# A four-layer graph network on one core: another order of the work ahead of the scatter, two ScalarE chunks in each fourth group, and another opening of the last layer

## The chip, the core and the metric

The kernel runs on one core of a Trainium2 chip. A core has five engines that work side by side: TensorE (PE in the rows, with its weight load PEld), VectorE (DVE), ScalarE (ACT), GpSimd (POOL) and SyncE (SP, here the queue that issues most DMAs). They meet only at semaphores: an instruction waits until a counter has reached a value that others raise. The metric is the device time of one execution in microseconds (us), lower is better.

## The reference, cut to what matters

625 nodes with 512 features, 20,000 edges. Each of four layers is `x = x + layer(relu(layernorm(x)))`.

```python
h = jnp.maximum(_layernorm(x), 0.0)
x = x + L0(h)   # GCN: deg by edge weight; agg = segment_sum(h@W_conv [src] * norm, dst); @ W_lin + b_lin
h = jnp.maximum(_layernorm(x), 0.0)
x = x + L1(h)   # SAGE: mean over incoming edges; h = mean @ W_l + b + x @ W_r; h * sigmoid(h)
h = jnp.maximum(_layernorm(x), 0.0)
x = x + L2(h)   # 4 blocks: conditioned norm, sparse attention (4 heads), conditioned norm, MLP
h = jnp.maximum(_layernorm(x), 0.0)
x = x + L3(h)   # GAT forward and backward (4 heads each), concat, @ W_fuse, batch norm, relu
```

The attention of L3 is, per direction, `e = leaky_relu(a_s[src] + a_d[dst], 0.2)`, a softmax over the edges of each target, and the weighted sum of `h[src]`. The conditioning of L2 comes from `silu(emb @ f_w1 + f_b1) @ f_w2 + f_b2`, with sines and cosines of node_vec1 in emb.

## The kernel before

The nodes lie in five tiles of 128 (NT = 5), the features in four (KT = 4). Matrices are kept as a high and a low part (fp32r), and a product of two of them is three matrix products.

**Ahead of the scatter** (span 0 to 34 us). DVE takes layer norm tile by tile: statistics, `first_norm(t)` (L2457), then PE turns the tile (`turn_first`, L1820), ACT makes the high part (`first_turned`, L1652), DVE the low part (`first_rest`, L2463), and PE multiplies it by W_conv (`own_features`, L1796; the last raises `big_full` for `hall`). In between, DVE adds two bias rows (L2514), splits the edge weights into three bf16 parts `w_part` (five operations, L2517 to L2520), and copies the identity into the accumulator (L2531, L2532). POOL makes the angles of the sines (L1433 to L1449, six steps on tile mask), the reciprocal deviations (`rstd_of`, L1409 and L1411), the low part of W_conv (`rest(Q_CONV)`, L1416), then adds the bias row to all five tiles of x (L1464), and clears paddings (L1469, L1472). ACT also makes sine, SiLU and high parts of weights.

**The scatter loop** (34 to 118 us). The edges come in NG = 40 groups of 512, each of CH = 4 chunks of 128. They become a dense 640 x 628 adjacency (weights and counts) by products of one-hot matrices in bf16. For a group, DVE makes the one-hot rows of the sources for three chunks (L2543, 128x628) and the one-hot rows of the targets (L2545, hot_dst), ACT the fourth chunk (Abs L1682, then Relu L1684), POOL multiplies hot_dst by the three weight parts (L1483, three operations), PE makes 60 small products (L2081, L2084), and DVE adds the result to the accumulator (L2554). HOT = 4 buffers turn, so DVE makes group n+3 and then adds group n. The loop body in code holds four groups, b = 0 to 3.

**Behind it**, DVE makes the two adjacencies and the degrees; POOL makes low parts of L1's left weights (L1416) and the power of the degrees (L1498), then the reciprocal deviations of L1's layer norm (L1409, L1411), for which DVE waits in its norm (L2457).

**The last layer** (785 to 890 us). PE makes the hidden features of both directions, `hidden(t)` (12 products, L1796), which ACT copies (L659). Then a loop over 8 heads and 5 source tiles (40 items): DVE combines two branches to scores (L1040, and L1003 for the row maxima), POOL and ACT make the exponentials (L632, L757), PE sums (L925, 4 products for an item). `target_rows(p)` turns four target rows for two heads (L843, ACT copies them at L669 and L675), `second_branch`, `first_branch` and `maxima` spread them over the partitions (L818). `idle_products(pe, bank, n)` makes n products of a tile of ones that nobody reads (L1807). PE's order here is written out by hand; `hidden(4)` comes last ahead of the loop.

SP loads L1's weights (Q_LEFT, Q_RIGHT) in pairs left and right; the first two of Q_RIGHT go to slots of the tile bias and wait for the adds of L1464.

## Time and profile before

| | us |
|---|---|
| median of 3 runs | 902.62 |
| lowest, highest | 901.32, 902.70 |
| the profiled execution | 900.32 |
| its span | 898.6 |
| PE busy | 837.1 (93%) |
| DVE busy | 644.9 (72%) |
| POOL busy | 516.5 (57%) |
| ACT busy | 459.7 (51%) |

The profile shows one execution. Times in its rows are from the start of the span; 1.7 us of the execution lie outside the span. Busy shares are means over stages with different limits, so a stage is read from its own stretch. An "x3" row holds three instructions in a row with one time from the first start to the last end; neighbouring instructions on an engine overlap a little at their ends, so the start of the next row is the better measure of what one costs. PEclk is the TensorE clock that was granted, 1.00 for 2.4 GHz and 0.50 for 1.2 GHz; its mean is 0.988.

### The profile page before, as it was taken

Reading aid. Unit: us, or ns where it says so; the run is one execution under the profiler, and the core shown is the slowest. Engines: PE = TensorE matmul, PEld = TensorE weight load, DVE = VectorE, ACT = ScalarE, POOL = GpSimd, SP = SyncE. Lnnn points to the kernel's source line nnn. Section 1 sums busy time; section 2 is a strip of 40 time slices with the busy share of each in tenths; the row PEclk is TensorE's granted clock in tenths of the full one; section 3 lists DMA queues with packets and bytes.
Section 4 is the critical chain, followed back from the end, with each engine's and each line's share of the span. In section 5 each row is a group of like instructions: output and inputs, shape, how many; then the busy total and the mean of one; then the engine's idle time right before and its main releaser. Section 6 shows DMA issues by size and latency. Waiting matters only on the chain.

```text
span 898.6 us, 18329 instructions
## 1 busy us (share of the span) xinstructions
PE 837.1 (93%) x6775; PEld 732.6 (82%) x6775; DVE 644.9 (72%) x1274; ACT 459.7 (51%) x771; POOL 516.5 (57%) x622
## 2 busy tenths in 40 slices
PE   3899999999999999999999999999999999998797
PEld 2798877779898878989887989888898988875466
DVE  8899988885575774476667366577546667689986
ACT  4787757244674233476134456424346634155664
POOL 7777744469532666743367853266684338447871
PEclk9999999999999999999999999999999999989989
DMA  5100011133200133300015310013230002100121
GB/s 135 37 0 0 0 48 26 60 102 110 59 2 5 31 109 91 109 13 2 12 44 159 89 54 12 1 36 98 81 113 20 1 1 83 36 1 31 45 60 58
DMA packets 49761, 44.34 MB, mean 49 GB/s; under 512 B 6013, under 2 KB 37439, under 8 KB 49698
## 3 DMA queue, kind: packets, MB, share of 16 engines
q1 hardware_dynamic: 47234, 39.72, 15.2%
q10 hardware_dynamic: 2464, 3.80, 1.5%
q8 instruction: 38, 0.62, 0.3%
q14 instruction: 25, 0.20, 0.1%
HBM read 42.04 MB, written 1.33 MB: 48 GB/s over the span
## 4 chain that ended last, share of the span: by engine, by line
PE 70%; DVE 16%; ACT 6%; issue 4%; DVEq 2%; POOL 1%; DMA 0%; SPq 0%; ACTq 0%
PE psum L1796 20%; PE psum L1790 18%; PE psum L1901 12%; PE psum L1871 6%; PE psum L1820 5%; PE psum L925 3%; DVE arena L2321 3%; ACT arena L1598 2%; PE psum L1844 2%; PE psum L866 1%; DVEq L2550 1%; DVE z L2543 1%; DVE arena L1003 1%; DVE stats L2444 1%; DVE hot_dst L2545 1%
## 5 line engine op out<-in xcount | busy, mean ns | idle before, releaser
L1345 POOL TENSOR_SCALAR acc<-acc,rden,flag 128x628 f32<-128x628 f32 x80 | 69.4, 868 | 119.4 <-DVE rden L2317 119.4
L1901 PE MATMUL psum<-ringw,arena 128*128 128x512 f32 (+1 forms) x480 | 119.3, 397 | 4.0 <-DVE arena L2329 2.5
L1796 PE MATMUL psum<-arena 128*128 128x384 f32 (+5 forms) x675 | 115.9, 325 | 1.1 <-DVE hot_dst L2694 1.1
L1790 PE MATMUL psum<-arena,ringw 128*128 128x314 f32 x768 | 114.2, 310 | 0.1
L1790 PEld LDWEIGHTS psum<-arena,ringw 128*128 128x128 f32 x768 | 112.9, 190 | 1.4 <-DVE arena L2294 1.1
L1796 PEld LDWEIGHTS psum<-arena 128*128 128x128 f32 (+1 forms) x675 | 104.9, 189 | 8.1 <-DVE hot_dst L2694 1.5
L1901 PEld LDWEIGHTS psum<-ringw,arena 128*128 128x128 f32 (+1 forms) x480 | 86.9, 186 | 25.6 <-DVE arena L2329 3.5
L1790 PE MATMUL psum<-arena 128*128 128x314 f32 (+1 forms) x480 | 87.8, 321 | 7.3 <-DVE arena L2321 6.7
L1790 PEld LDWEIGHTS psum<-arena 128*128 128x128 f32 (+1 forms) x480 | 70.4, 187 | 15.8 <-DVE arena L2321 14.1
L1416 POOL TENSOR_TENSOR ringw<-raw,ringw 128x512 fp32r<-128x512 f32 x56 | 71.7, 1291 | 19.3 <-ACT ringw L1639 15.4
L2294 DVE SCALAR_TENSOR_TENSOR arena<-psum,cols,arena 128x628 fp32r<-128x628 f32 x32 | 27.9, 871 | 70.6 <-ACT arena L1580 70.5
L1820 PE MATMUL psum<-ident,acc 128*128 128x128 f32 (+1 forms) x528 | 75.3, 274 | 0.2
L2321 DVE TENSOR_TENSOR arena<-psum,arena 128x640 fp32r<-128x640 f32 x80 | 65.0, 817 | 14.5 <-ACT arena L1598 14.5
L1416 POOL TENSOR_TENSOR ringw<-xn,ringw 128x512 fp32r<-128x512 f32 x49 | 64.9, 1329 | 16.2 <-ACT ringw L1639 16.1
L1483 POOL TENSOR_TENSOR hot_dst<-hot_dst,w_part 128x160 bf16<-128x160 bf16 x120 | 58.2, 512 | 26.2 <-DVE hot_dst L2545 26.2
L1593 ACT ACTIVATE acc<-acc,nsmax 128x628 f32<-128x628 f32 x80 | 65.2, 815 | 13.3 <-DVE nsmax L2312 12.9
L1820 PEld LDWEIGHTS psum<-ident,acc 128*128 128x128 f32 (+1 forms) x528 | 61.7, 140 | 8.0 <-DVE arena L2294 1.2
L1409 POOL TENSOR_SCALAR veps<-mv 128x1 f32<-128x1 f32 x60 | 13.6, 227 | 90.7 <-DVE mv L2448 89.0
L2312 DVE CUSTOM_DVE_ANT_0 acc<-psum,mask 128x628 f32<-128x628 f32 x80 | 63.7, 801 | 0.0
L1529 ACT ACTIVATE arena<-psum 128x512 fp32r<-128x512 f32 x40 | 23.8, 594 | 73.8 <-PE psum L1820 58.9
L1796 PE MATMUL psum<-arena,ringw 128*128 128x314 f32 x384 | 58.5, 310 | 2.3 <-DVE arena L2211 2.3
L1871 PE MATMUL psum<-ringw,arena 128*128 128x512 f32 x240 | 58.7, 395 | 0.9 <-DVE arena L2211 0.6
(310 smaller groups left out, 1907.0 us busy)
## 6 DMA issues: line engine op xcount, KB each, us to landing
raw<-in_L_gnn_m_w SPq DMA_DIRECT2D x16, 256.0 KB
xn<-in_L_gnn_m_w SPq DMA_DIRECT2D x16, 256.0 KB
raw<-in_L_gnn_wv SPq DMA_DIRECT2D x8, 256.0 KB
xn<-in_L_gnn_wv SPq DMA_DIRECT2D x8, 256.0 KB
raw<-in_L_gnn_wq SPq DMA_DIRECT2D x8, 256.0 KB
xn<-in_L_gnn_wq SPq DMA_DIRECT2D x8, 256.0 KB
raw<-in_L_gnn_wk SPq DMA_DIRECT2D x8, 256.0 KB
xn<-in_L_gnn_wk SPq DMA_DIRECT2D x8, 256.0 KB
```

Source lines behind the costliest of these rows:

```text
L1345: g.tensor_scalar(pbuf[:, k % 4, 0:NW], pbuf[:, k % 4, 0:NW], rden[:, k:k + 1], flag[:, 1, k % NT:k % NT + 1], ALU.mult, ALU.mult).then_in ...
L1416: g.tensor_tensor(to[1], staged[slot(n)], to[0].bitcast(F32), ALU.subtract).then_inc(split_done, 1)
L1483: ins = g.tensor_tensor(hot_dst[:, b, :, (i + 1) * WIN:(i + 2) * WIN], hot, w_part[:, i, :, bass.ds(gr, 1)].broadcast_to([P, CH, WIN]), AL ...
L1593: act.activation(pbuf[:, k % 4, 0:NW], pbuf[:, k % 4, 0:NW], ACT.Exp, bias=nsmax[:, k:k + 1], scale=-1.0, accum_out=den[:, k:k + 1]).then_ ...
L1790: ins = pe.matmul(big[buf(u)][0:l.shape[1], h, 0:HW], l, r[:, h * HW:(h + 1) * HW], start=(i == 0), stop=(i == len(terms) - 1))
L1796: ins = pe.matmul(to, l, r, start=(i == 0), stop=(i == len(terms) - 1))
L1820: ins = pe.transpose(bflat(u)[0:KEYS[k], k * P:(k + 1) * P], src[:, k * P:k * P + KEYS[k]], ident[:, :])
L1871: ins = pe.matmul(brow(u), l, r, start=(k == 0 and i == 0), stop=(k == KT - 1 and i == 2))
L1901: ins = pe.matmul(brow(ROWBLK[f"{name}{t}"])[0:KEYS[t], :], l, r, start=(pieces[0] + i == 0), stop=(pieces[-1] == KT - 1 and i == len(term ...
L2294: dve.scalar_tensor_tensor(wide(to[:, 1, h, :]), bwide(u), bqk[:, i, bass.ds(it * KT + h, 1)], wide(f32(to[:, 0, h, :])), ALU.add, ALU.sub ...
L2312: dve.tensor_tensor_reduce(wide(pbuf[:, k % 4, :]), bwide(u), wide(mask[:, t, :]), -DH ** -0.5, 3e38, ALU.add, ALU.min, nsmax[:, k:k + 1]) ...
L2321: dve.tensor_tensor(pT[:, 1, :, t * P:(t + 1) * P], bflat(u).rearrange("p (k n) -> p k n", k=NT), f32(pT[:, 0, :, t * P:(t + 1) * P]), ALU ...
```

## The change

Five parts.

- **A, order ahead of the scatter.** DVE splits the weights right after `first_norm(3)`, ahead of the bias addition, `first_rest(2)` and `first_norm(4)`. The copies of the identity go to ACT, which also makes ones_r and two high parts ahead of `first_turned(2)`. DVE no longer waits for `hall` ahead of its loop, and does the small pick operation (L2576) before the loop instead of behind it. POOL makes `rest(Q_CONV)` ahead of the third and fourth rstd_of, and the five bias additions to x move behind the loop: two behind `left_rest(0, 1)`, three behind `left_rest(2, 3)`, ahead of L1's `rstd_of`. PE turns the last tile after `own_features(1)`, makes z1, then `own_features(2)` to `(4)`, and 2 products of ones instead of 4. SP loads L1's weights in another order, the first of Q_RIGHT into z.
- **B, the scatter loop.** In the group b = 3 ACT makes two chunks and DVE two (instead of one and three); a third scratch lies in xn.
- **C.** Products of ones: 6 instead of 7 behind the loop, 3 instead of 1 at L1's third tile.
- **D, the opening of the last layer.** The products of ones (1, 3 and 3) go. `hidden(4)` is made in two halves in their place, ahead of `second_branch(0)` and `second_branch(1)`; ACT copies Hf3 ahead of `second_branch(1)` and Hf4 behind it; 5 products of ones instead of 6 ahead of the loop.
- **E, the last layer's loop.** Four times 4 products of ones, one ahead of `target_rows(3)`'s wait and one behind each ACT read of target rows at n = 5, 15, 25.

```diff
-        hot_abs = [mask[:, NT - 1, :].bitcast(BF16)[:, b * NP:(b + 1) * NP] for b in range(2)]
+        def own_chunks(b):
+            return CH - 1 - (b == HOT - 1)
+        hot_abs = [... for b in range(2)] + [xn[:, 1, D - NP // 2:D].bitcast(BF16)]
...
             second_branch(0)
+            hidden("f", 3)
             second_branch(1)
-            for t in range(3, NT):
-                hidden("f", t)
+            hidden("f", 4)
...
+                if p == NJ // 2 - 1:
+                    idle_products(pe, 0, 4)
                 pe.wait_ge(c_up, 2 * p + 2)
...
-            pe.wait_ge(h_read, 2 * NT - NROW)
-            spare = 2 * NBIG + ROW3[f"Hf{NT - 1}"] % NROW
-            idle_products(pe, spare, 1)
             target_rows(0)
-            idle_products(pe, spare, 3)
+            hidden(4, range(0, KT // 2))
             second_branch(0)
-            idle_products(pe, spare, 3)
+            hidden(4, range(KT // 2, KT))
...
             first_branch(1)
-            hidden(4)
-            idle_products(pe, 2 * NBIG, 6)
+            idle_products(pe, 2 * NBIG, 5)
...
+                for p in range(1, NJ // 2):
+                    if n == 2 * NT * p - 5:
+                        pe.wait_ge(misc_read, MISC[f"vt{p}"] + 1)
+                        idle_products(pe, 0, 4)
...
+            g.wait_ge(dstep, 9)
             step(g.tensor_tensor(r, part, ph, ALU.add))
...
             rstd_of(2, 2)
+            rest(Q_CONV, ringpart(Q_CONV))
+            rstd_of(3, 3)
...
             for k in range(2):
                 left_rest(k)
+            for t in range(2):
+                bias_added(t)
             g.wait_ge(w_up, 1)
...
             for k in range(2, KT):
                 left_rest(k)
+            for t in range(2, NT):
+                bias_added(t)
...
+                        for j in range(own_chunks(b), CH):
+                            act.activation(hot_abs[n][:, 0:NW], iota16[:, 0:NW], ACT.Abs, ...)
+                            act.wait_ge(hot_abs_up, ...)
+                            ins = act.activation(hot_src[b][:, j, 0:NW], hot_abs[n][:, 0:NW], ACT.Relu, ...)
+                        ins.then_inc(hot_act_up, 1)
...
-            dve.wait_ge(big_full, BIG0["hall"] + 1)
...
-                    for j in range(CH - 1):
+                    for j in range(own_chunks(b)):
```

How the instructions stand on DVE from the last layer norm tiles to the loop; xn is the normed tile, w_part the split weights, the rows at L2543 and L2572 the first one-hot chunks. Before:

```order
L2514 TENSOR_TENSOR bias<-psum,bias 128x512
L2463 SCALAR_TENSOR_TENSOR arena<-psum,arena 128x4x128
L2457 TENSOR_SCALAR xn<-x,mv,rstd 128x512
L2517 CAST w_part<-edge_col 128x160
L2519 TENSOR_TENSOR edge_col<-edge_col,w_part 128x160
L2520 CAST w_part<-edge_col 128x160
L2519 TENSOR_TENSOR edge_col<-edge_col,w_part 128x160
L2520 CAST w_part<-edge_col 128x160
L2463 SCALAR_TENSOR_TENSOR arena<-psum,arena 128x4x128 x2
L2531 COPY acc<-ident 128x4x128
L2532 COPY acc<-ident 128x128
L2537 TENSOR_LOAD span_i
```

After:

```order
L2546 CAST w_part<-edge_col 128x160
L2548 TENSOR_TENSOR edge_col<-edge_col,w_part 128x160
L2549 CAST w_part<-edge_col 128x160
L2548 TENSOR_TENSOR edge_col<-edge_col,w_part 128x160
L2549 CAST w_part<-edge_col 128x160
L2556 TENSOR_TENSOR bias<-psum,bias 128x512
L2498 SCALAR_TENSOR_TENSOR arena<-psum,arena 128x4x128
L2492 TENSOR_SCALAR xn<-x,mv,rstd 128x512
L2498 SCALAR_TENSOR_TENSOR arena<-psum,arena 128x4x128
L2561 TENSOR_TENSOR pick<-fcol,pick 128x1
L2498 SCALAR_TENSOR_TENSOR arena<-psum,arena 128x4x128
L2566 TENSOR_LOAD span_i
```

The five operations on the weights stand ahead of the last norm now, and the two copies are gone from this engine.

On POOL behind the scatter loop, from the low parts of L1's left weights (ringw) to the first reciprocal deviation. Before:

```order
L1416 TENSOR_TENSOR ringw<-raw,ringw 128x512 x2
L1498 TENSOR_TENSOR degs<-degs,half 128x2
L1498 TENSOR_TENSOR degs<-degs,half 128x3
L1416 TENSOR_TENSOR ringw<-raw,ringw 128x512 x2
L1409 TENSOR_SCALAR veps<-mv 128x1
```

After:

```order
L1434 TENSOR_TENSOR ringw<-raw,ringw 128x512 x2
L1484 TENSOR_TENSOR x<-x,bias 128x512 x2
L1520 TENSOR_TENSOR degs<-degs,half 128x2
L1520 TENSOR_TENSOR degs<-degs,half 128x3
L1434 TENSOR_TENSOR ringw<-raw,ringw 128x512 x2
L1484 TENSOR_TENSOR x<-x,bias 128x512 x3
L1427 TENSOR_SCALAR veps<-mv 128x1
```

Two additions stand ahead of the power, three ahead of the first deviation.

On PE in the opening of the last layer; 128x256 are hidden features, 36x128 the turned target rows, 128x314 from arena the spread branches, ones_r the products of ones, and hot_dst the first item of the loop. Before:

```order
L1796 MATMUL psum<-ringw,arena 128x256 x12
L1807 MATMUL psum<-ones_r 128x512
L843 MATMUL psum<-ident,iota 36x128 x5
L1807 MATMUL psum<-ones_r 128x512 x3
L818 MATMUL psum<-arena 128x314 x2
L1807 MATMUL psum<-ones_r 128x512 x3
L818 MATMUL psum<-arena 128x314 x8
L1796 MATMUL psum<-ringw,arena 128x256 x12
L1807 MATMUL psum<-ones_r 128x512 x6
L925 MATMUL psum<-hot_dst,acc 128x314 x4
```

After:

```order
L824 MATMUL psum<-ringw,arena 128x256 x12
L857 MATMUL psum<-ident,iota 36x128 x5
L824 MATMUL psum<-ringw,arena 128x256 x6
L830 MATMUL psum<-arena 128x314 x2
L824 MATMUL psum<-ringw,arena 128x256 x6
L830 MATMUL psum<-arena 128x314 x8
L1840 MATMUL psum<-ones_r 128x512 x5
L938 MATMUL psum<-hot_dst,acc 128x314 x4
```

The twelve products of the fifth tile stand where six of the products of ones stood, and between the last spread and the first item only five products of ones are left.

## Rows read from the trace of the kernel before

**Rows 1.** The page: the chain that ended last, by engine.

```profile
PE 70%; DVE 16%; ACT 6%; issue 4%; DVEq 2%; POOL 1%; DMA 0%; SPq 0%; ACTq 0%
```

**Rows 2.** Timeline of DVE ahead of the scatter: start, us, engine, line, operation, [idle before, releaser].

```profile
23.27 0.23 DVE L2517 CAST w_part<-edge_col 128x160 bf16<-128x160 f32 x1
...
23.89 1.21 DVE L2520 CAST w_part<-edge_col 128x160 bf16<-128x160 f32 x1
...
27.58 0.68 DVE L2463 SCALAR_TENSOR_TENSOR arena<-psum,arena 128x512 fp32r<-128x512 f32 x1
28.99 0.69 DVE L2463 SCALAR_TENSOR_TENSOR arena<-psum,arena 128x512 fp32r<-128x512 f32 x1 [0.73 <-ACT arena L1652]
29.59 1.01 DVE L2531 COPY acc<-ident 128x512 f32<-128x512 f32 x1
...
33.72 0.97 DVE L2543 TENSOR_SCALAR mask<-iota,edge_col 128x628 bf16<-128x628 f16 x3 [2.92 <-issue]
```

**Rows 3.** Timeline of POOL ahead of the scatter.

```profile
21.54 1.28 POOL L1416 TENSOR_TENSOR ringw<-raw,ringw 128x512 fp32r<-128x512 f32 x1
...
23.62 6.41 POOL L1464 TENSOR_TENSOR x<-x,bias 128x512 f32<-128x512 f32 x5
```

**Rows 4.** Timeline of PE ahead of the scatter, and its first product of the loop.

```profile
22.97 2.05 PE L1796 MATMUL psum<-ringw,arena 128*128 128x256 f32 x8 [1.89 <-DVE arena L2463]
...
30.30 2.16 PE L1796 MATMUL psum<-ringw,arena 128*128 128x256 f32 x16
...
37.07 0.20 PE L2081 MATMUL psum<-hot_dst,mask 128*128 128x80 bf16 x1 [3.67 <-ACT z L1684]
```

**Rows 5.** Timeline of DVE in the scatter loop: its start, and single operations of one steady group.

```profile
35.92 0.58 DVE L2545 TENSOR_TENSOR hot_dst<-iota,edge_col 128x160 bf16<-128x160 f16 x1
...
96.57 0.58 DVE L2543 TENSOR_SCALAR z<-iota,edge_col 128x628 bf16<-128x628 f16 x1
97.07 0.31 DVE L2545 TENSOR_TENSOR hot_dst<-iota,edge_col 128x160 bf16<-128x160 f16 x1
97.31 0.56 DVE L2554 TENSOR_TENSOR acc<-psum,acc 128x400 f32 x1
```

**Rows 6.** Timeline of POOL in that group: its third product.

```profile
96.43 0.54 POOL L1483 TENSOR_TENSOR hot_dst<-hot_dst,w_part 128x160 bf16<-128x160 bf16 x1
```

**Rows 7.** Timeline of ACT: two one-hot pairs at the loop's start, without a wait.

```profile
33.81 0.80 ACT L1682 ACTIVATE mask<-iota,edge_col 128x628 bf16<-128x628 f16 x1
...
35.28 0.80 ACT L1682 ACTIVATE mask<-iota,edge_col 128x628 bf16<-128x628 f16 x1
```

**Rows 8.** Stretches of the scatter: us, busy (x count) of PE, PEld, DVE, ACT, POOL, PEclk, DMA share, GB/s.

```profile
38.40:41.40 3.00, 3.00 (x73) 3.00 (x70) 3.00 (x8) 1.54 (x2) 2.39 (x6) 0.50 0.00 0
45.00:53.00 8.00, 7.41 (x252) 7.22 (x248) 8.00 (x21) 6.69 (x10) 5.65 (x12) 1.00 0.00 0
```

**Rows 9.** Timelines of POOL, DVE and PE at L1's layer norm.

```profile
131.00 0.19 POOL L1409 TENSOR_SCALAR veps<-mv 128x1 f32<-128x1 f32 x1 [2.40 <-DVE mv L2448]
...
132.69 0.51 DVE L2457 TENSOR_SCALAR xn<-x,mv,rstd 128x512 f32<-128x512 f32 x1
...
137.93 0.66 PE L1820 MATMUL psum<-ident,xn 128*128 128x128 f32 x4 [1.06 <-DVE xn L2457]
```

**Rows 10.** Timeline of PE in the last layer's opening.

```profile
805.35 2.90 PE L1807 MATMUL psum<-ones_r 128*128 128x512 f32 x6 [0.56 <-ACT acc L659]
```

**Rows 11.** Timeline of DVE in the last layer: the waits for PE.

```profile
810.07 0.87 DVE L1040 SCALAR_TENSOR_TENSOR hot_dst<-psum,edge_col,bias 128x628 f32<-128x628 f32 x1 [2.57 <-PE psum L925]
...
860.09 0.87 DVE L1040 SCALAR_TENSOR_TENSOR raw<-psum,edge_col,bias 128x628 f32<-128x628 f32 x1 [0.37 <-PE psum L925]
...
868.42 0.87 DVE L1040 SCALAR_TENSOR_TENSOR raw<-psum,edge_col,bias 128x628 f32<-128x628 f32 x1 [0.19 <-PE psum L925]
```

**Rows 12.** Timeline of PE in the last layer's loop: the last of its long waits.

```profile
853.12 1.62 PE L925 MATMUL psum<-hot_dst,acc 128*128 128x314 f32 x4 [2.04 <-ACT z L693]
```

**Rows 13.** A stretch of the last layer's loop, columns as in rows 8.

```profile
854.00:861.00 7.00, 7.00 (x15) 4.17 (x14) 6.59 (x7) 3.75 (x6) 5.42 (x3) 0.52 0.42 128
```

More of the change, by code:

```diff
@@ L505, in slot, with place @@
             return (n - S_COND) % STAGE if n >= S_COND else n % OUTER
+        def place(n):
+            return z[:, NT - 1, :] if n == Q_RIGHT[0] else staged[slot(n)]
         def ld_count(n):
@@ L805, in hidden_and_own, with hidden @@
                        sum([parts(tile_of(yT, k, t), [wb[:, s, k, :] for s in range(2)]) for k in range(KT)], [])).then_inc(h_full, 1)
-            def hidden(t):
+            def hidden(t, ks=range(KT)):
                 u = ROW3[f"Hf{t}"]
-                pe.wait_ge(h_read, NT + t - NROW + 1)
-                pe.wait_ge(split_done, S_L3 + 4)
+                if ks[0] == 0:
+                    pe.wait_ge(h_read, NT + t - NROW + 1)
+                    pe.wait_ge(split_done, S_L3 + 4)
                 def weight(k):
                     return [r[:, (k % 2) * w:(k % 2 + 1) * w] for r in ringpart(RING_L3 + k // 2)]
-                row_mm(pe, brow(u)[:, 0:w], sum([parts(tile_of(yT, k, t), weight(k)) for k in range(KT)], [])).then_inc(h_full, 1)
+                for k in ks:
+                    for i, (l, r) in enumerate(parts(tile_of(yT, k, t), weight(k))):
+                        ins = pe.matmul(brow(u)[:, 0:w], l, r, start=(k == 0 and i == 0), stop=(k == KT - 1 and i == 2))
+                if ks[-1] == KT - 1:
+                    ins.then_inc(h_full, 1)
             def spread(to, pick, rows):
@@ L1460, in _, with bias_added @@
             g.wait_ge(hot_init, 3)
-            for t in range(NT):
+            def bias_added(t):
                 g.wait_ge(xn_up, t + 1)
@@ L1638, in high @@
                 act.wait_ge(raw_ld[slot(n)], ld_count(n) + it * LD_PERBLK)
-                act.activation(to, staged[slot(n)], ACT.Copy).then_inc(shi_up, 1)
+                act.activation(to, place(n), ACT.Copy).then_inc(shi_up, 1)
             act.dma_start(tmp64[0][:, 0:N], a["node_vec1"].rearrange("n o -> o n").broadcast_to([2 * NF, N])).then_inc(noise_ld, 16)
@@ L1660, in _ @@
             first_turned(1)
+            act.wait_ge(scat_read, HOT)
+            act.wait_ge(scat_full, HOT)
+            step_w = ACCW * 2 + P
+            diag = acc[:, ACCW:ACCW + (NT - 1) * step_w].rearrange("p (t n) -> p t n", n=step_w)[:, :, 0:P]
+            act.activation(diag, ident[:, :].unsqueeze(1).broadcast_to([P, NT - 1, P]), ACT.Copy).then_inc(acc_up, 1)
+            act.activation(w_acc[:, NT - 1, (NT - 1) * P:NP], ident[:, :], ACT.Copy).then_inc(acc_up, 1)
+            act.activation(ones_r[:, :], ones[:, :], ACT.Copy).then_inc(ones_up, 1)
+            for m in range(2, 4):
+                high(m, ringpart(m)[0])
             first_turned(2)
@@ L1670, in _ @@
             act.activation(wide_all(silu), z1, ACT.Silu, bias=fcol[0:C16, 3:4]).then_inc(silu_up, 1)
-            act.activation(ones_r[:, :], ones[:, :], ACT.Copy).then_inc(ones_up, 1)
-            for m in range(2, 4):
-                high(m, ringpart(m)[0])
             act.wait_ge(w_ready, 2)
@@ L2046, in _ @@
             row_mm(pe, brow(ROW0["brow"])[:, :], parts([bc_hl[:, 0, :], bc_hl[:, 1, :]], ringpart(Q_LIN))).then_inc(row_full, 1)
-            for t in range(2, NT):
+            for t in range(2, 4):
                 turn_first(t)
                 own_features(t - 2)
+            turn_first(4)
             pe.wait_ge(row_read, ROW0["brow"] + 1)
```

62 lines of the change are left out of this document (31 added, 31 removed).

## The prediction

> **What bounds the kernel now.** I read the chain of waits first: PE carries 70% of the span, DVE 16%, ACT 6% [rows 1]. The middle of the kernel is PE's, and the change leaves it alone. It works in three stretches, so each is read from its own rows. Ahead of the scatter loop the timeline of DVE shows no long gap until 30.80: it works through norms and the splitting of the weights, and its first one-hot chunk starts at 33.72 [rows 2]. In the loop DVE is busy for 8.00 of 8.00 us and PE for 7.41 [rows 8], so DVE sets the pace, PE just under it. In the last layer DVE feeds the loop over heads; it waits 2.57 us for PE's first sums [rows 11], because PE comes to them behind products of ones that start at 805.35 and last 2.90 at half the clock [rows 10]. From 854 to 861 PE is busy throughout at a granted clock of 0.52 [rows 13], and DVE waits for it five times until 868.42, 1.7 us together, first and last shown [rows 11].
>
> **Start of the loop (part A).** Three terms, all on DVE. First the weights: the five operations take 4.31 us now, 23.27 to 27.58, but the first two take 0.62 (23.27 to 23.89) and only those beside POOL's additions take 1.2 each [rows 2, 3]. With those additions gone, casts at 0.26 and subtractions at 0.36 give 1.5 in all: -2.8. Second, the copies of the identity, 29.59 to 30.80 (33.72 less 2.92), go to ACT: -1.2 [rows 2]. Third, the wait of 2.92: DVE waits for PE's last product with W_conv, whose block ends at 32.46 (30.30 and 2.16), and its first chunk follows 1.26 later [rows 2, 4]. Without that wait only reading the number of passes is left, some 1.1 to 1.3: -1.7. Together -5.7.
>
> Something must not be late in their place. The last low part has to wait for PE's turning and ACT's high part. PE's first block with W_conv stands at 22.97 only because POOL makes W_conv's low part from 21.54 to 22.82 [rows 3, 4]; POOL now makes it some 4 to 5 us earlier, so PE's block starts at about 20.6, the last tile is turned at about 25.7, ACT is through at 26.5 and DVE at 27.1, and with 1.1 behind that the first chunk comes at 28.2; if the reading overlaps the last operation, at 27.6. I take 27.9, which is -5.8, with -5.3 and -6.6 as bounds. ACT's copies of the identity stand in a gap in which it waits for PE anyway, and they, like all of ACT's and POOL's moved steps, must be done only by 28. PE's first scatter product came 3.35 us behind DVE's first chunk, at 37.07 [rows 4]. PE's blocks with W_conv end at 32.46 now and 2 to 3 us earlier then; ACT's first pair must follow SiLU, so I put PE's first product near 31. DVE's first addition comes only behind the one-hot rows of four groups; two of them took 2.7 us (33.72 to the end of the row at 35.92) [rows 2, 5], so it is not before 33.3, and PE needs 2.47 for a group even at half clock [rows 8]: +0.2 (0 to 0.7). Two products of ones fewer lie in a wait: nothing. SP's new order of loads has 80 us of cover.
>
> **The loop (part B).** In one of four groups DVE makes one chunk less. A chunk beside POOL costs 0.50 (96.57 to 97.07) [rows 5]. That is not all gained. POOL's third product runs from 96.43 to 96.97 [rows 6], so the last chunk met it, and the target rows behind it ran alone in 0.31. With two chunks the target rows come 0.5 earlier and meet that product; there they take 0.58, as they do at 35.92 [rows 5]. So a fourth group gives 0.50 - 0.27 = 0.23, and ten of them -2.3. The other end is the full 0.50: -5.0. I take the first, since the row at 35.92 is the same operation in the same meeting. The Trainium skill (Trainium Architecture — The Big Picture, "What this means for kernel authors") says that of the engines only VectorE and GpSimd contend for a port pair in SBUF, and that it is an exclusive lock and not a bandwidth split; by that rule too the loser waits for the whole product, and the trace agrees (0.58 against 0.31). It speaks against the full gain.
>
> ACT must keep up. A pair costs 1.47 (33.81 to 35.28) [rows 7]; five are 7.35 against 8.16 - 0.23 = 7.93 for four groups. PE needs 7.41 of 8.00 us now, so 7.56 of 7.93 [rows 8]. Both fit, by 0.6 and 0.4 us per four groups, and ACT has three groups of lead by the four buffers.
>
> **Behind the loop (parts A and C).** POOL is free from 128.60 (131.00 less 2.40) and now makes three additions there, at 6.41/5 = 1.28 each [rows 3, 9]: until 132.44, where its deviation now starts at 131.00, so that is 1.44 late. DVE's norm starts at 132.69, about 0.85 behind the end of that deviation (0.83 for its two steps), so 0.6 to 0.7 is left: +0.7 (0 to 1.4). The first two additions lie in POOL's wait ahead of the power, and delay it by 0.1 at most, against 0.2 that DVE gains by the pick moved away. One product of ones fewer is nothing; two more at the third tile take 0.8 in a wait of 1.06 [rows 9].
>
> **Last layer, opening (part D).** With the twelve products of the fifth tile in place of six products of ones, PE comes to the first item some 3 us earlier. What can be gained is DVE's wait, 2.57 [rows 11]; then DVE itself is late next. Each half (six products) stands for three products of ones and may shift second_branch by 0.3 either way. ACT's copy between the branches takes 0.4, of which I count nothing: it stands where ACT waits for PE's next branch. I take -2.4, bounds -2.0 and -2.65.
>
> **Last layer, loop (part E).** PE waits 2.04 us ahead of 853.12 [rows 12], the longest of four such gaps in the loop. After the last of them the clock is at 0.52, its lower level, for 7 us [rows 13]. Four products of ones, 0.95 us at full clock, now stand in each. If they keep the clock, the stretch goes: DVE's waits of 1.7 are the near bound, and 3.3 the far one (7 us of products at half clock, less what DVE hides). I take -2.5. If the clock still falls the term is zero. The Trainium skill (TensorE: Matmul & The Clock Gate, Part 1) says that the default state is throttled and activity releases it. By that rule the products serve, and the term stands; a fall all the same would leave it out.
>
> **The sum.** -5.8 + 0.2 - 2.3 + 0.7 - 2.4 - 2.5 = -12.1. The profiled execution took 900.32, which gives 888.2; the median of the runs is 2.3 higher, 902.62, so I say 890.5.
>
> **The rivals.**
>
> 1. The clock falls in the last layer's loop all the same: the 2.04 us gap is only half filled, and the clock of a stretch is not set by that gap alone. Then part E gives nothing: 893.0.
>
> 2. The chunk saved in the loop is gained in full, since POOL and DVE shift against each other: 2.7 more, 887.8. For it speaks that a moved phase may find the chunks alone; against it that POOL starts only behind DVE's target rows, so the phase is tied.
>
> 3. ACT sets the loop's pace. A pair waits between Abs and Relu, and the row's 1.47 has no wait for PE in it; if that costs a quarter of a us each time, a pair is 1.73 (an estimate), and five are 8.65 where DVE had 8.16, +0.5 for four groups, +4.9 for the loop instead of -2.3: 897.7. Against it: 1.47 was seen back to back.
>
> 4. The start is not DVE's: PE's and ACT's chain to the last low part, or the first group on PE, takes back half. Then part A's first term is -3 instead of -5.8, and the change does not do there what it seems to: 893.3.
>
> 5. On the slower side: PE's clock. At 38.40 to 41.40 it was at 0.50, and PE got through 73 operations in 3.00 us, where at full clock it was 252 in 8.00 [rows 8]. A group's 60 products take 2.47 at half clock, above DVE's 2.04. If the new rhythm, in which PE waits for ACT's second chunk in each fourth group, kept the clock down through the loop, a group would cost 0.43 more: forty are 17, and with the loop's gain of 2.3 lost too the kernel is at 890.5 + 19.5 = 910. It decides from 24 groups at half clock: 24 x 0.43 = 10.3 and their lost share of 2.3. Against it: PE is busy 0.93 of the time and would be more so.
>
> **How the numbers follow.** The forecast 0.50, the clock in the last layer 0.19, the full chunk 0.11, ACT's pace 0.07, the start 0.09, the clock in the loop 0.04. The range goes from 886.5 (the full chunk and a start at its better bound) to 895.5 (the clock in the last layer with the worse bounds of the start, of POOL's additions and of the first addition); it leaves out rivals 3 and 5 and a little beyond both ends, under 2 in 10. A measurement of this kernel tells some 0.2%, 1.8 us, from no change. All cases but the last and mishaps in several terms at once are below 900.8: faster 0.95, within 0.2% 0.02, slower 0.03.
>
> **What would show it.** DVE's first chunk at 27.9 in the timeline, with the five operations on the weights at 0.2 to 0.4 each. In the loop, a period of 2.04 in three groups and 1.81 in the fourth, target rows of 0.58 there, DVE still busy throughout, ACT with short waits. Behind it, POOL's first deviation right behind three additions and DVE waiting 0.6 for it. In the last layer no 2.57 wait ahead of the sixth score, and a granted clock of 1.00 from 854 to 861 by the old count. I am wrong if DVE shows gaps in the loop that ACT ends, if the first chunk stands at 30 or later, or if the half clock only moves elsewhere.

## The result, and the profile after

| | before | after |
|---|---|---|
| median, us | 901.97 (4 runs, 897.75 to 902.70) | 889.94 (4 runs, 889.44 to 890.62) |
| ratio after / before | | 0.9877, 95% interval 0.9845 to 0.9909 |
| the profiled execution, us | 900.32 | 889.44 |
| its span, us | 898.6 | 887.7 |
| PE, DVE, ACT, POOL busy, us | 837.1, 644.9, 459.7, 516.5 | 833.4, 640.2, 472.2, 516.5 |

The change makes the kernel 1.2% faster; 890.5 was predicted. The executions of the kernel before spread over 5 us, those of the kernel after over 1.2; that spread is nearly as large as the largest term of the prediction, and the medians have to be read with it. The two traces, compared at the same instruction of DVE, give this account of the 10.9 us between the spans:

| DVE reaches | before | after | difference | gained or lost in between |
|---|---|---|---|---|
| first one-hot chunk | 33.72 | 27.81 | -5.91 | -5.9 |
| last target rows of the loop | 113.38 | 104.84 | -8.54 | -2.6 |
| first norm of L1 | 132.69 | 125.46 | -7.23 | +1.3 |
| first score of the last layer | 801.38 | 794.42 | -6.96 | +0.3 |
| fifth score | 810.07 | 800.47 | -9.60 | -2.6 |
| the reciprocal at the loop's end | 872.20 | 861.57 | -10.63 | -1.0 |
| end of the span | 898.6 | 887.7 | -10.9 | -0.3 |

**Ahead of the loop.** The timeline of DVE in the kernel after, with start, us, engine, line, operation and [idle before, releaser], answers to [rows 2].

```profile
21.89 0.24 DVE L2546 CAST w_part<-edge_col 128x160 bf16<-128x160 f32 x1
...
22.52 0.24 DVE L2549 CAST w_part<-edge_col 128x160 bf16<-128x160 f32 x1
22.80 0.33 DVE L2548 TENSOR_TENSOR edge_col<-edge_col,w_part 128x160 f32<-128x160 f32 x1
23.16 0.24 DVE L2549 CAST w_part<-edge_col 128x160 bf16<-128x160 f32 x1
...
26.57 0.69 DVE L2498 SCALAR_TENSOR_TENSOR arena<-psum,arena 128x512 fp32r<-128x512 f32 x1 [0.31 <-ACT arena L1676]
27.81 0.97 DVE L2572 TENSOR_SCALAR mask<-iota,edge_col 128x628 bf16<-128x628 f16 x3 [0.55 <-issue]
```

The five operations on the weights take 1.4 us, none of them 1.2 any more; the wait ahead of the first chunk is 0.55 instead of 2.92. PE's first scatter product, foretold near 31, comes 3.1 us behind the chunk, where [rows 4] has 3.35:

```profile
30.91 0.20 PE L2116 MATMUL psum<-hot_dst,mask 128*128 128x80 bf16 x1 [0.36 <-POOL hot_dst L1503]
```

**The loop.** A group in which DVE makes two chunks, on DVE, then 8 us of the loop with the columns of [rows 8]:

```profile
104.02 0.90 DVE L2572 TENSOR_SCALAR z<-iota,edge_col 128x628 bf16<-128x628 f16 x2
104.84 0.58 DVE L2574 TENSOR_TENSOR hot_dst<-iota,edge_col 128x160 bf16<-128x160 f16 x1
```

```profile
45.00:53.00 8.00, 7.65 (x249) 7.34 (x245) 8.00 (x20) 7.81 (x12) 5.89 (x13) 1.00 0.00 0
```

The target rows take 0.58 there, as foretold from [rows 5]. DVE still has no gap, PE is at 7.65 and ACT at 7.81 of 8.00: three engines are within 5% of each other. ACT is catching up in this stretch: its pairs follow each other without a wait, at the 1.47 us of [rows 7], until 69 us, and from then on it waits; in the round of four groups from 72.30 to 80.23 it is busy for 7.40 of 7.93.

**Behind the loop.** DVE, then POOL:

```profile
109.24 0.58 DVE L2583 TENSOR_TENSOR acc<-psum,acc 128x400 f32 x1 [0.51 <-PE psum L2119]
109.74 0.90 DVE L2599 CAST base_i<-base_f 1x40 int32<-1x40 f32 x1
...
125.46 0.55 DVE L2492 TENSOR_SCALAR xn<-x,mv,rstd 128x512 f32<-128x512 f32 x1 [0.55 <-POOL rstd L1429]
```

```profile
109.31 2.52 POOL L1484 TENSOR_TENSOR x<-x,bias 128x512 f32<-128x512 f32 x2
...
120.70 3.80 POOL L1484 TENSOR_TENSOR x<-x,bias 128x512 f32<-128x512 f32 x3
124.59 0.19 POOL L1427 TENSOR_SCALAR veps<-mv 128x1 f32<-128x1 f32 x1
```

The norm waits 0.55 for the deviation that three additions delay; that was in the sum. What was not: a cast of 40 numbers takes 0.90 us, 0.7 more than in the kernel before, and it stands beside POOL's first additions.

**The last layer.** PE in the opening, DVE's fifth score, and the clock of 795 to 800:

```profile
795.31 2.50 PE L1840 MATMUL psum<-ones_r 128*128 128x512 f32 x5
797.93 2.75 PE L938 MATMUL psum<-hot_dst,acc 128*128 128x314 f32 x8
```

```profile
800.47 0.87 DVE L1053 SCALAR_TENSOR_TENSOR hot_dst<-psum,edge_col,bias 128x628 f32<-128x628 f32 x1
```

```profile
795.00:800.00 5.00, 4.88 (x14) 3.00 (x14) 5.00 (x11) 1.73 (x4) 4.57 (x4) 0.66 0.01 2
845.00:862.00 17.00, 15.64 (x63) 10.62 (x63) 17.00 (x19) 13.26 (x21) 14.07 (x8) 1.00 0.29 71
```

The clock still falls in the opening, from 2.4 to 1.2 GHz for part of the stretch, but no wait stands ahead of the fifth score now, where [rows 11] has 2.57. (The prediction's signs call it the sixth score; the row at 810.07 is the fifth.) At the loop's end the clock stays at 1.00 where [rows 13] has 0.52.

### The profile page after: what moved, and what is told of

The parts are those of the page before. It is cut to its first block, busy times and chain, and to the rows that moved or that the text cites. A ratio compares the mean times of both kernels' runs of the same rounds, so it can differ in the third digit from the quotient of the medians.

```text
span 887.7 us, 18402 instructions
## 1 busy us (share of the span) xinstructions
PE 833.4 (94%) x6782; PEld 728.7 (82%) x6782; DVE 640.2 (72%) x1262; ACT 472.2 (53%) x793; POOL 516.5 (58%) x622
## 4 chain that ended last, share of the span: by engine, by line
PE 63%; DVE 19%; ACT 5%; issue 4%; DVEq 3%; POOL 2%; DMA 2%; SPq 1%; POOLq 0%
PE psum L1829 18%; PE psum L1823 18%; PE psum L1934 11%; PE psum L1904 6%; PE psum L1853 5%; DVE arena L2356 3%; ACT arena L1622 2%; DVE arena L1016 2%; PE psum L1877 1%; DVEq L2579 1%; PE psum L880 1%; DVE z L2572 1%; PE psum L938 1%; DVE mask L2572 1%; DVE stats L2479 1%
## 5 line engine op out<-in xcount | busy, mean ns | idle before, releaser
L2329 DVE SCALAR_TENSOR_TENSOR arena<-psum,cols,arena 128x628 fp32r<-128x628 f32 x32 | 27.9, 871 | 71.5 <-ACT arena L1604 71.5
```

The lines of the kernel that those rows point to most:

```text
L2329: dve.scalar_tensor_tensor(wide(to[:, 1, h, :]), bwide(u), bqk[:, i, bass.ds(it * KT + h, 1)], wide(f32(to[:, 0, h, :])), ALU.add, ALU.sub ...
```

## The experiments

All but two were timed several times beside runs of the kernel before; w_late and hall_wait stand on one execution each. "The changed kernel" is the kernel after.

### undo_b and swap_add: what one chunk in the loop is worth

```diff
-            return CH - 1 - (b == HOT - 1)
+            return CH - 1
... (with ACT's scratch and the counts of its waits to match)
```

> The changed kernel with part B undone: DVE makes three one-hot chunks in every group, ACT one. Theory (in the fourth group the target rows meet POOL's third product, so that only 0.24 of a chunk's 0.50 us is saved): every group takes 2.04 us again, target rows are 0.31 us in all of them, the loop is 2.4 us longer than the changed kernel's (77.0 us from DVE's first chunk to the end of its last target rows), the time about 892.3. Rival (a chunk is worth its full 0.50, and the rest of the gain was lost elsewhere, at the loop's start or end): 5 us longer, about 895.

Measured: 892.36 (891.46 to 893.85). From the first chunk at 27.55, the last target rows come at 107.29:

```profile
107.29 0.31 DVE L2574 TENSOR_TENSOR hot_dst<-iota,edge_col 128x160 bf16<-128x160 f16 x1
```

That is 79.7 us against 77.0, and 2.4 us by the medians. The full price of 0.50 a chunk (5 us) is ruled out.

```diff
-                        hot(gi * HOT + b + HOT - 1, (b + HOT - 1) % HOT)
-                        add(gi * HOT + b, b)
+                        made, at = gi * HOT + b + HOT - 1, (b + HOT - 1) % HOT
+                        sources(made, at)
+                        if at == HOT - 1:
+                            add(gi * HOT + b, b)
+                            targets(made, at)
+                        else:
+                            targets(made, at)
+                            add(gi * HOT + b, b)
```

`sources` and `targets` are the two halves of `hot`: the one-hot chunks, and the target rows.

> The changed kernel with one swap in DVE's loop: in the group with two chunks the addition comes ahead of the target rows, so that these start when POOL's third product is over. Theory of the shared port: the target rows there take 0.31 instead of 0.58, the addition (PSUM and SBUF) is not slowed, and a round of four groups takes 7.45 instead of 7.69 us: 2.4 us less in ten rounds, about 887.5. Rival (PE or ACT is the limit now; PE is busy 7.65 of 8.00 us and ACT's five pairs are 7.35): DVE shows waits for PE instead, and less than 1 us is gained, 889 to 890.

Measured: 889.75 (889.39 to 890.05), no gain. A round of four groups takes 7.89 to 7.91 us (from 56.35 to 64.26 and to 72.15), against 7.93 in the changed kernel (from 56.44 to 64.37 and to 72.30). The 7.69 that the expectation started from was a slip: the prediction had 7.93, 8.16 less 0.23, and the trace has it. Neither side of the expectation is what happened. DVE in one round of swap_add:

```profile
64.26 0.90 DVE L2576 TENSOR_SCALAR z<-iota,edge_col 128x628 bf16<-128x628 f16 x2
65.08 0.56 DVE L2589 TENSOR_TENSOR acc<-psum,acc 128x400 f32 x1
65.56 0.31 DVE L2580 TENSOR_TENSOR hot_dst<-iota,edge_col 128x160 bf16<-128x160 f16 x1
65.79 1.38 DVE L2576 TENSOR_SCALAR mask<-iota,edge_col 128x628 bf16<-128x628 f16 x3
67.10 0.57 DVE L2580 TENSOR_TENSOR hot_dst<-iota,edge_col 128x160 bf16<-128x160 f16 x1
```

DVE has no wait for PE. The target rows of the swapped group are down to 0.31, and those of the next group are up to 0.57: POOL starts the swapped group's products later, since they wait for its target rows, and its third now meets the next group's. POOL makes twelve products a round in either order. Alone, DVE's eleven chunks, four target rows and four additions of a round would take 6.1 us (an estimate from 0.29, 0.24 and 0.48 each, start to start); the other 1.8 are some 0.15 for each product of POOL, in this order and in the old one (12 chunks, 6.4 of 8.16). So taking a chunk from DVE frees about what the chunk takes when alone: 0.23 a round measured, 0.29 by the start of the loop, where three take 0.88 from 33.72 to 34.60. Moving operations about freed less than 0.05 a round.

### act_six: the next limit in the loop

```diff
-            return CH - 1 - (b == HOT - 1)
+            return CH - 1 - b % 2
... (with ACT's scratch and the counts of its waits to match)
```

> The changed kernel with ScalarE making two chunks in two of four groups: six pairs a round. Theory (a pair costs 1.47 us and ScalarE, at 7.8 of 8.0 us busy, is at its limit): a round takes 8.82 instead of 7.89 us, DVE waits for PE and PE for ScalarE's chunks, the loop is some 8 to 9 us longer, time about 898. Rival (ScalarE has slack and DVE's one chunk less a round is worth another 0.25): 2.5 us shorter, about 887.5.

Measured: 899.24 (899.05 to 900.60), 9.3 above the changed kernel. The stretch of 61 to 69 us, and a wait of DVE in it:

```profile
61.00:69.00 8.00, 6.70 (x218) 6.39 (x215) 6.37 (x17) 7.84 (x12) 4.79 (x11) 1.00 0.00 0
```

```profile
66.49 0.57 DVE L2583 TENSOR_TENSOR acc<-psum,acc 128x400 f32 x1 [0.55 <-PE psum L2119]
```

ScalarE sets the pace: 6 x 1.47 = 8.8 us a round against 7.93. Five pairs are the most it can take, and the third rival of the prediction is what one pair more brings.

### w_late and hall_wait: the terms ahead of the loop

w_late puts the five operations back behind the last norm:

```diff
-            step(dve.tensor_copy(w_part[:, 0, :, :], w_col[:, :, :]))   # and the four behind it
             u = ROW0["brow"]
...
             first_norm(4)
+            step(dve.tensor_copy(w_part[:, 0, :, :], w_col[:, :, :]))   # and the four behind it
             first_rest(3)
```

> The changed kernel with the five operations on the edge weights put back behind the last layer norm tile. Theory (they took 4.3 us in the kernel before because POOL's additions ran beside them, and their place is nothing): they take 1.2 to 1.5 us here too, DVE's first chunk comes 0 to 0.8 us later than at 27.8. Rival (their place, next to the last tile's copies, is what made them slow): two casts and a subtraction at 1.2 each again, first chunk at 30 or later.

```profile
24.30 0.24 DVE L2555 CAST w_part<-edge_col 128x160 bf16<-128x160 f32 x1
...
27.42 0.97 DVE L2572 TENSOR_SCALAR mask<-iota,edge_col 128x628 bf16<-128x628 f16 x3 [0.44 <-issue]
```

Measured: 889.91. The cast that took 1.21 in [rows 2] takes 0.24 at the old place too, and the first chunk comes at 27.42. That is no gain over 27.81: the kernels with the same order ahead of the loop have it anywhere from 27.55 (undo_b) to 28.54 (undo_d). So the place in DVE's order is worth nothing that can be measured here; it was POOL's additions that cost 2.9 us, and their going is the gain.

```diff
             dve.wait_ge(hot_init, 3)
+            dve.wait_ge(big_full, BIG0["hall"] + 1)
```

> The changed kernel with DVE's wait for PE's last product with W_conv put back ahead of its loop. Theory (third term, this wait ended last in the kernel before and would again): PE ends these products at 30.1, DVE's first chunk comes 1.2 later, at 31.2 to 31.4 instead of 27.8, the time 3.4 longer. Rival (DVE's lead is not used, since PE's first scatter product at 30.9 sets the pace): the first chunk is late but the last of the loop hardly, under 1 us longer.

```profile
31.61 0.68 DVE L2573 TENSOR_SCALAR mask<-iota,edge_col 128x628 bf16<-128x628 f16 x2 [4.06 <-issue]
```

Measured: 893.49. The first chunk is 3.8 late, far outside the 27.4 to 28.5 of the others, the last target rows too (108.62 against 104.84), and the time 3.6. DVE's lead is carried through the loop in full. It also corrects the split of the first term: with this wait the rest of part A brings only 33.72 - 31.61 = 2.1, and that is PE's doing, whose products with W_conv end at 30.37 here and at 32.46 in the kernel before; dropping the wait brings the other 3.8.

### adds_moved and adds_spread: what the moved additions cost

```diff
+            for t in range(2):
+                bias_added(t)
             g.wait_ge(w_ready, 2)              # ahead of the scatter loop
...
-            for t in range(2):
-                bias_added(t)
             g.wait_ge(w_up, 1)
...
+            for t in range(2, NT):
+                bias_added(t)
             g.wait_ge(h0lo_up, NT)
             for k in range(2, KT):
                 left_rest(k)
-            for t in range(2, NT):
-                bias_added(t)
```

> The changed kernel with the bias additions placed elsewhere on POOL: two ahead of the scatter loop (POOL is idle from 25.8 to 29.2 us), three in its wait behind the power of the degrees (idle for 3.9 us, they take 3.8). Theory (behind the loop DVE's small cast takes 0.90 instead of 0.16 us since it meets an addition, and the norm waits 0.55 us for the late deviation): both go, 1.3 us, but DVE's additions of the adjacency (two inputs in SBUF, 0.82 each) now meet POOL's and give back 0 to 1: between 888.5 and 889.9. Rival (the cast's 0.90 has another cause): the cast still takes 0.7 or more, and only the 0.55 goes.

Measured: 892.88 (892.01 to 894.56), 2.9 above the changed kernel. DVE and POOL:

```profile
110.08 0.17 DVE L2599 CAST base_i<-base_f 1x40 int32<-1x40 f32 x1
...
113.94 1.23 DVE L2624 SCALAR_TENSOR_TENSOR degs<-degs 128x3 f32<-128x3 f32 x1
115.21 1.87 DVE L2607 TENSOR_TENSOR arena<-acc,arena 128x640 fp32r<-128x640 f32 x1
117.00 1.62 DVE L2611 SCALAR_TENSOR_TENSOR arena<-hot_dst,degs,arena 128x128 fp32r<-128x128 f32 x2
```

```profile
113.87 4.34 POOL L1484 TENSOR_TENSOR x<-x,bias 128x512 f32<-128x512 f32 x3
```

The cast is back at 0.17, so its 0.90 was the meeting with an addition; the rival falls. But three additions in POOL's own idle time stretch three groups of DVE's, which take 0.16, 0.82 and 0.61 in the changed kernel, by 1.0 each, 3.1 in all where I allowed 1 at most. POOL's idle time was not free: DVE was working in SBUF in it. Less the 1.3 that came back, this is the 1.8 us by which the first score of the last layer is late (796.25 against 794.42); in the profiled execution the last layer adds 0.6 (67.8 from the first score to the reciprocal, against 67.2).

The next version takes both lessons, two additions ahead of the scatter loop, and the other three where DVE works on PSUM and statistics:

```diff
-            for t in range(2, NT):
-                bias_added(t)
+            bias_added(2)
             for t in range(NT):
                 rstd_of(LN_L1 + t, NT + t)
+                if t in (1, 2):
+                    bias_added(t + 2)
```

> The changed kernel with the five bias additions placed anew on POOL: two ahead of the scatter loop, one behind the last low parts of L1's left weights, and one each behind the second and third deviation, so that none stands ahead of the first deviation but one and none meets the adjacency additions. Theory: the small cast takes 0.17 instead of 0.90 us, the norm's wait of 0.55 us goes, and the loop starts 0.2 later: -1.1 against the changed kernel's profile up to L1's norm, time about 888.9, unless the clock in the last layer takes it back. Rival (DVE's later updates of x wait for the two last additions): a wait of 0.5 us or more ahead of L2672 and no gain.

```profile
110.11 0.17 DVE L2600 CAST base_i<-base_f 1x40 int32<-1x40 f32 x1
...
124.48 0.51 DVE L2493 TENSOR_SCALAR xn<-x,mv,rstd 128x512 f32<-128x512 f32 x1
```

Measured: 888.57 (888.37 to 889.36), the lowest median of the study, 1.4 below the changed kernel's, whose runs stand in another round. Against the runs of the kernel before that stand beside each, the ratios are alike (0.9876, 0.9855 to 0.9898, and 0.9877), since those vary by more than the effect; so the gain rests on the trace: the norm starts at 124.48 instead of 125.46, without a wait, and the first score of the last layer at 793.56 instead of 794.42. That is as far as the trace bears it out. In the profiled executions the last layer gives it back (the reciprocal stands at 861.35 against 861.57, the spans are 887.6 and 887.7), so a gain in the time is not shown. The two additions ahead of the loop are not quite free either: the pick beside them takes 0.92 instead of 0.15.

### undo_d, undo_e, before_d, before_e, ab_only: the last layer

undo_d puts the old opening back into the changed kernel (the inverse of D in the diff above), undo_e takes out the 16 products of ones (the inverse of E), ab_only does both. before_d and before_e put D or E alone into the kernel before.

> The changed kernel with the old opening of the last layer: hidden(4) behind the first branches, products of ones 1, 3, 3 and 6. Theory: DVE's wait ahead of its fifth score is back at 2.5 to 2.7 us and nothing else changes, about 892.6. Rival (the wait was there, but part of it is given back later in the loop by other waits): less than 1.5 us longer, below 891.5.

> The changed kernel without the 16 products of ones in the last layer's loop. From the two traces: the clock falls to 0.5 for some 7 us behind the last long gap, DVE waits for PE for 2.4 us again, but its mask products and the wide addition (which took 2.05, 1.27 and 2.14 us beside POOL) get shorter again by about 1.3 us: 1.0 to 1.3 us longer, about 891.2. Rival (the term as predicted, 2.5): 892.5. Rival (the products do nothing, the clock stays up anyway): 890.0.

> The kernel before with part D alone (the fifth tile in halves ahead of the second branches, three groups of products of ones gone). Two theories on the wait of 2.57 us ahead of DVE's fifth score in the kernel before. One: it is the order's, and part D removes it: 2.6 us faster than before in nearly every execution, about 899.5. Other (undoing D in the changed kernel cost nothing, and there the clock stayed at 1.00 through the opening): the wait is the half clock's, and D helps only where the clock falls in the opening: the profile shows whether PEclk fell there; where it did, DVE has no wait there all the same and gains 2.6, where it did not, nothing. Then the executions lie between 897 and 902 as before's do, with the median lower by 0 to 2.6.

> The kernel before with part E alone (16 products of ones in the last layer's loop). Theory (E keeps the clock up in the loop, and the loop's falls are what varies from one execution to the next): faster by 1.0 to 1.3 us by what the two traces showed in that stretch, and the clock at 1.00 from 812 on; DVE's wait of 2.6 us in the opening stays if the clock falls there. About 900.8, with less spread. Rival (E is worth the whole 4.7 us that undoing it cost in the changed kernel): 897.4.

> The changed kernel with both D and E undone, so the last layer of the kernel before behind the new order and loop. Theory (the falls of the clock in the last layer decide, and E prevents them): executions on two levels, one near 890 where no fall comes or it is hidden, one 3 to 9 us higher where it is not, median 893 to 898. Rival (D and E are worth their predicted 2.4 and 2.5 whatever the clock does): every execution near 894.5 to 895.

| kernel | D | E | behind the old or new start and loop | median | executions |
|---|---|---|---|---|---|
| after | yes | yes | new | 889.94 | 889.4 to 890.6 |
| undo_d | no | yes | new | 889.83 | 889.1 to 890.7 |
| undo_e | yes | no | new | 894.61 | 890.0, 890.7, 890.8, 898.5, 898.5, 898.8 |
| ab_only | no | no | new | 893.35 | 891.6 to 894.0 |
| before_e | no | yes | old | 897.55 | seven from 896.0 to 897.8, five from 899.5 to 900.9 |
| before_d | yes | no | old | 903.80 | five from 896.5 to 898.7, seven from 903.5 to 905.2 |
| before | no | no | old | 901.28 (23 runs beside before_d) | 897.5 to 904.6 |

The prediction's two terms, 2.4 and 2.5 whatever else happens, do not survive this table. By the medians E is worth 3.5 where D is absent (ab_only against undo_d), 3.7 in the kernel before, and 4.7 beside D (undo_e). D is worth nothing beside E. Without E the medians with D are the higher ones, by 1.3 (undo_e against ab_only) and 2.5 (before_d against before), both well within the spread of their executions. The theories of the expectations missed with it: undoing D was to cost 2.5, undoing E 1.0 to 1.3, before_d was to be no slower than the kernel before, before_e was to come at 900.8 and came at its rival's 897.4, and ab_only, in its median as expected, was to show two levels and shows one.

What the profiles have in common is the clock. undo_d, the old opening, has the products of ones at full clock and no fall (and its four executions a mean clock of 0.998 or 0.999):

```profile
797.89 1.60 PE L1845 MATMUL psum<-ones_r 128*128 128x512 f32 x6 [0.57 <-ACT acc L666]
```

```profile
795.00:800.00 5.00, 4.36 (x24) 3.52 (x24) 5.00 (x10) 2.30 (x5) 4.22 (x3) 1.00 0.01 2
```

Its products of ones take 1.60 us where [rows 10] has 2.90, and DVE has no wait. So the wait of 2.57 was made by the half clock; the order alone did not make it. With the clock down, the order matters. before_e has the fall and the old order:

```profile
805.00:810.00 5.00, 4.43 (x11) 3.31 (x11) 2.76 (x6) 3.43 (x5) 3.64 (x3) 0.52 0.01 2
```

```profile
810.31 0.87 DVE L1046 SCALAR_TENSOR_TENSOR hot_dst<-psum,edge_col,bias 128x628 f32<-128x628 f32 x1 [2.55 <-PE psum L931]
```

before_d has the same fall and the new order. Its fifth score comes without a wait, 6.05 us behind the first instead of 8.68; but the clock falls twice again in the loop, from 816 to 824 and from 837 to 845, and DVE waits there:

```profile
805.00:810.00 5.00, 4.79 (x9) 3.20 (x10) 4.96 (x10) 2.61 (x4) 5.00 (x4) 0.50 0.01 2
815.00:820.00 5.00, 3.73 (x8) 2.17 (x9) 3.79 (x8) 3.75 (x6) 3.94 (x4) 0.69 0.26 70
835.00:840.00 5.00, 3.28 (x8) 1.82 (x9) 5.00 (x12) 3.52 (x7) 4.94 (x5) 0.73 0.28 69
```

```profile
807.73 0.87 DVE L1040 SCALAR_TENSOR_TENSOR hot_dst<-psum,edge_col,bias 128x628 f32<-128x628 f32 x1
...
818.17 0.87 DVE L1040 SCALAR_TENSOR_TENSOR hot_dst<-psum,edge_col,bias 128x628 f32<-128x628 f32 x1 [0.98 <-PE psum L925]
...
821.48 0.87 DVE L1040 SCALAR_TENSOR_TENSOR xn<-psum,edge_col,bias 128x628 f32<-128x628 f32 x1 [1.71 <-PE psum L925]
```

undo_e shows the same falls, one in the opening (0.59 in 800 to 805) and two in the loop, from 811 to 822 and from 831 to 839; its profiled execution is one of the long ones:

```profile
810.00:815.00 5.00, 5.00 (x12) 3.12 (x12) 2.52 (x6) 3.01 (x5) 2.81 (x2) 0.59 0.39 134
830.00:835.00 5.00, 3.98 (x8) 2.25 (x9) 4.45 (x10) 3.61 (x6) 4.60 (x4) 0.64 0.27 69
```

From the first score to the reciprocal the changed kernel takes 67.2 us, undo_e 76.1 and before_d 74.7. Of the ten profiled kernels that have E, none has a fall from 810 to 870 us; all four without it have one or two. So E is worth what the falls that it prevents would have cost, and that differs from one execution to the next: with D in place 0 to 9 us (undo_e). The three short executions of undo_e are not shown to be free of falls: their mean granted clock is 0.991, between the 0.984 of the long ones and the 0.994 to 0.999 of the changed kernel, and none of them was profiled. D removes 2.6 us up to the fifth score where a fall stands in the opening, and nothing otherwise; no median shows the 2.6.

D without E is also where the loop falls twice (undo_e, before_d), while the kernels with neither fall once: before from 854 to 861, and ab_only from 827 to 831. That D itself, which takes eight of thirteen products of ones out of the opening and brings the loop's first sums forward, invites these falls is a rival that the table supports and no run isolates. The profile of ab_only is not a typical one either: it is the shortest of its six executions (891.58), with a mean clock of 0.996 where the other five have 0.990. What sets off a fall the runs do not settle; the layer starts at another time in each.

## Why the prediction was right, and where it was not

**The first chunk (part A):** 27.9 predicted, 27.81 measured. PE's first block with W_conv came at 21.0 (20.6 foretold), ACT's last high part ended at 26.5 (26.5), DVE's last low part at 27.3 (27.1). The three terms were right in sum and not in how they share it: -2.8 for the weights measured -2.9, and w_late shows its cause as argued; but they are not to be added freely. With the wait for `hall` left in, all the rest of part A would have brought 2.1 (hall_wait), and that by PE's earlier products alone; the wait is worth 3.8 and not 1.7. That the first chunk was met within 0.1 is in part luck, since it moves by 1 us between kernels that are alike up to there. A term that ends a stretch must be priced against what the stretch would wait for without the others.

**The loop (part B):** -2.3 predicted, -2.6 in the trace, -2.4 by undo_b; three groups take 2.04 and the fourth 1.81, as foretold. The 0.2 for DVE's waiting at its first addition did not come. The Trainium skill (Trainium Architecture — The Big Picture, "What this means for kernel authors") calls the port pair of VectorE and GpSimd an exclusive lock; the target rows at 0.31 alone and 0.58 beside a product agree, and swap_add shows that the cost follows the product, not the place.

**Behind the loop:** +0.7 predicted, +1.3 measured. The delay of the deviation was 0.55 to 0.63, as worked out. The step that failed is "the first two additions lie in POOL's wait ahead of the power, and delay it by 0.1 at most": it looked at who waits for POOL, and not at what DVE does meanwhile. DVE's cast there took 0.7 more.

**The opening of the last layer (part D):** -2.4 predicted, -2.6 in the traces. The mechanism was half right. The step "because PE comes to them behind products of ones that start at 805.35 and last 2.90 at half the clock", of DVE's wait of 2.57, named both causes, and the sum then treated the second as fixed. It is not: undo_d has none of it. As a statement on the median of many executions the term is too large: undoing D cost nothing.

**The loop of the last layer (part E):** -2.5 predicted, -1.0 in the traces, and 3.5 to 4.7 by the medians, so the term was wrong in both readings, once above its far bound of 3.3. The mechanism held: no fall in the loop with E. In the traces DVE's waits for PE went, all 1.7 us of them and 0.7 for ACT besides. What was missed is who was late next. The timeline of DVE in the kernel after:

```profile
851.65 2.05 DVE L1058 TENSOR_TENSOR raw<-raw,mask 128x628 f32<-128x628 f32 x1
...
855.96 1.27 DVE L1058 TENSOR_TENSOR acc<-acc,mask 128x628 f32<-128x628 f32 x1
...
859.50 2.14 DVE L1067 SCALAR_TENSOR_TENSOR arena<-z,cols,arena 128x628 fp32r<-128x628 f32 x1
```

POOL beside them:

```profile
851.51 1.52 POOL L601 TENSOR_TENSOR z<-z 128x628 f32<-128x628 f32 x1
...
855.05 1.52 POOL L639 TENSOR_TENSOR acc<-acc,mask 128x628 f32<-128x628 f32 x1
...
858.94 2.03 POOL L639 TENSOR_TENSOR raw<-raw,mask 128x628 f32<-128x628 f32 x1 [0.33 <-DVE raw L1053]
```

The same operations of DVE in the kernel before:

```profile
862.36 0.88 DVE L1045 TENSOR_TENSOR raw<-raw,mask 128x628 f32<-128x628 f32 x1
...
866.21 0.80 DVE L1045 TENSOR_TENSOR acc<-acc,mask 128x628 f32<-128x628 f32 x1
...
870.74 1.33 DVE L1054 SCALAR_TENSOR_TENSOR arena<-z,cols,arena 128x628 fp32r<-128x628 f32 x1 [0.73 <-ACT arena L717]
```

Without its waits DVE comes to these while POOL is at products of its own, and the three take 1.17, 0.47 and 0.81 us more, 2.45 together. Counted from start to start they cost 2.1 more and the waits that went 3.1, which leaves the 1.0. No run takes POOL's work away there, so that the 2.45 are the meeting is read from the rows and not shown by an experiment. But it is not the products of ones that slow them: before_d, undo_e and ab_only, without E and without a fall at the loop's end, have them at 2.04, 1.28 and 2.13 as well.

**The sum:** 12.1 predicted for the two profiled executions, 10.9 measured: 1.5 too much in part E and 0.6 behind the loop, against 0.8 too little in parts A, B and D together. The medians are 12.0 apart all the same, because the profiled execution of the kernel before was 1.6 below its median and that of the kernel after 0.5. So the median was met within 0.6 us with a sum that was 1.2 too high on the traces; the spread of the kernel before made up for it, and that is luck. The medians divide otherwise as well: A to C together are 7.9 (ab_only against the kernel before beside it, 901.28) where the sum had 7.2, D and E together 3.4 (893.35 against 889.94) where it had 4.9. The ends of the range are wider than the terms named for them give, which are 887.0 and 894.7.

**The rivals.** The clock in the last layer's loop (first) did not happen in any profile with E. The full chunk (second) is excluded by undo_b and swap_add. ScalarE's pace (third) is not reached, with 0.58 us a round to spare, and is reached with one pair more. The fourth, a start that PE and ACT hold back, did not happen. PE's clock in the scatter (fifth) was 1.00 from 31 us on.

## What to carry to other kernels

Price a moved instruction on GpSimd by what VectorE does beside it: three additions in GpSimd's idle time cost VectorE 3.1 us, and the same three, one slot each beside work on PSUM and statistics, nothing that the trace shows. When a profile's wait stands in a stretch of half clock, ask first what the wait would be at full clock, and look at many executions: a fall that comes in some of them has another price in the median than in the one that was profiled. A wait that is removed is worth the distance to the next late event, so of several terms that end at one point only the sum is known.

## What the runs showed of the hardware

- A small operation is not small beside the other engine of the pair: a cast of 1x40 numbers took 0.90 us beside a 128x512 addition on GpSimd and 0.17 without; one on 128x3 numbers took 1.23 instead of 0.16, one on 128x1 (the pick, L2562 in adds_spread) 0.92 instead of 0.15.
- Work on PSUM and statistics was not slowed: in adds_spread the statistics at 125.69 take 0.69 us beside POOL's addition from 125.38 to 126.68, as they do elsewhere without one.
- The granted clock of TensorE is not a property of the instruction order alone. The same undo_e gave three executions near 890.5, at a mean clock of 0.991, and three near 898.6, at 0.984, and with the same instructions in the opening of the last layer, which begins some 7 us earlier in one than in the other, the profiled executions had it at 1.00 (undo_d) and at 0.52 (before_e).
